# Output products of the experts in two halves, first keys by operands, three loads at other places

## What is computed

```
x = x + tanh(g_xattn) * Attn(layernorm(x), ctx, ctx)     # 16 heads of 32
    q = (query @ Wq.T) * 32**-0.5;  k = key @ Wk.T;  v = value @ Wv.T
    scores = sigmoid(q k^T);  o = scores @ v;  out = o @ Wo.T
x = x + tanh(g_ffn) * FFN(layernorm(x))
    tokens = x.reshape(8, 448, 512)                       # two batches per expert
    h = gelu(tokens @ w1[e] + b1[e])                      # 512 -> 2048
    y = h @ w2[e] + b2[e]                                 # 2048 -> 512
```

## Time and profile before

| | us |
|---|---|
| median of 3 runs | 1655.48 |
| lowest and highest | 1653.58, 1656.01 |
| the profiled execution | 1653.71 |
| its span in the profile | 1652.0 |
| PE busy | 1644.5 |
| PEld busy | 1452.0 |
| VectorE busy | 804.8 |
| ScalarE busy | 796.9 |
| POOL busy | 175.9 |

### The profile page before, as it was taken

The page is one execution under the profiler, slowest core; times in us unless marked ns, Lnnn a source line. Parts: engine busy times, 40 slices in busy tenths (PEclk is TensorE's granted clock), DMA queues, the critical chain, the costliest instruction groups (busy, mean ns, idle before and its releaser), DMA issues.

```text
span 1652.0 us, 30322 instructions
## 1 busy us (share of the span) xinstructions
PE 1644.5 (100%) x11460; PEld 1452.0 (88%) x11460; DVE 804.8 (49%) x1388; ACT 796.9 (48%) x1087; POOL 175.9 (11%) x261
## 2 busy tenths in 40 slices
PE   9999999999999999999999999999999999999999
PEld 8888888888888888888888887999999999999998
DVE  5545444443443443544443443674746565555544
ACT  6655555555555555555555556333333333333332
POOL 1212111111111111111121120000000000000000
DMA  8977687777677787786776775535344352526251
GB/s 278 265 216 217 198 222 204 195 226 206 192 220 213 194 224 204 193 237 187 210 225 186 210 227 149 203 125 180 124 168 150 131 183 98 188 93 227 94 171 48
DMA packets 195691, 309.03 MB, mean 187 GB/s; under 512 B 27088, under 2 KB 153616, under 8 KB 195568
## 3 DMA queue, kind: packets, MB, share of 16 engines
q1 hardware_dynamic: 173632, 229.43, 49.4%
q0 software_dynamic: 21936, 77.94, 13.6%
HBM read 228.44 MB, written 78.84 MB: 186 GB/s over the span
## 4 chain that ended last, share of the span: by engine, by line
PE 97%; DMA 2%; DVE 0%; SPq 0%; ACT 0%; issue 0%; POOLq 0%; DVEq 0%; ACTq 0%
PE fill_ps L686 31%; PE scores_ps L872 19%; PE fill_ps L853 14%; PE scores_ps L728 10%; PE heads_ps L745 9%; PE fill_ps L695 6%; PE heads_ps L853 5%; PE fill_ps L696 3%; DMA k_st<-k_scr 1%; DMA k_scr<-k_stage 0%; DMA probs<-WKT_in 0%; DMA part_scr<-part 0%; PE scores_ps L695 0%; SPq L404 0%; PE scores_ps L696 0%
## 5 line engine op out<-in xcount | busy, mean ns | idle before, releaser
L872 PE MATMUL scores_ps<-ctx_hl,wK 128*128 128x448 f32 x1536 | 316.6, 362 | 0.0
L872 PEld LDWEIGHTS scores_ps<-ctx_hl,wK 128*128 128x128 f32 x1536 | 288.1, 188 | 19.8
L686 PE MATMUL fill_ps<-ctx_hl,wK 128*128 128x500 f32 (+1 forms) x1560 | 287.6, 334 | 0.4 <-DVE wK L1093 0.4
L686 PE MATMUL fill_ps<-wV,ctx_hl 128*125 128x512 f32 x1152 | 280.5, 395 | 0.2 <-DVE k_stage L1201 0.2
L686 PEld LDWEIGHTS fill_ps<-ctx_hl,wK 128*128 128x128 f32 x1560 | 236.2, 189 | 31.8 <-issue 6.0
L686 PEld LDWEIGHTS fill_ps<-wV,ctx_hl 128*125 128x125 f32 x1152 | 208.9, 186 | 48.1 <-DVE k_stage L1201 0.4
L853 PE MATMUL fill_ps<-wQ,wV 128*128 128x448 f32 x1152 | 243.4, 365 | 0.0
L853 PEld LDWEIGHTS fill_ps<-wQ,wV 128*128 128x128 f32 x1152 | 216.0, 188 | 17.2 <-issue 0.4
L911 ACT ACTIVATE probs<-scores_ps 125x896 f32<-125x896 f32 x192 | 176.8, 921 | 86.7 <-PE scores_ps L728 54.4
L728 PE MATMUL scores_ps<-q_st,k_st 96*125 96x224 f32 x1536 | 200.7, 273 | 2.1 <-DMA k_st<-k_scr 2.1
L728 PEld LDWEIGHTS scores_ps<-q_st,k_st 96*125 96x125 f32 x1536 | 188.0, 188 | 16.0 <-issue 6.2
(11 more groups left out here) (120 smaller groups left out, 1706.1 us busy)
## 6 DMA issues: line engine op xcount, KB each, us to landing
k_st<-k_scr SPq DMA_DIRECT2D x576, 125.0 KB, 3.9
v_sb<-w_in SPq DMA_DIRECT2D x92, 512.0 KB, 4.6
k_scr<-k_stage POOLq DMA_DIRECT2D x62, 500.0 KB, 4.5
ctx_raw<-ctxT_in SPq DMA_DIRECT2D x48, 500.0 KB, 4.6
q_st<-q_scr SPq DMA_DIRECT2D x192, 112.0 KB, 4.0
k_scr<-k_stage POOLq DMA_DIRECT2D x68, 250.0 KB, 4.1
probs<-w_in SPq DMA_DIRECT2D x32, 512.0 KB, 3.6
q_scr<-q_stage POOLq DMA_DIRECT2D x64, 224.0 KB, 5.0
```

The lines of the kernel that those rows point to most:

```text
L686: last = pe.matmul(out_, lhsT(kt, a), rhs(kt, c), start=(kt == 0 and t == 0), stop=(kt == KT - 1 and t == 2))
L872: last = pe.matmul(y_ps[:, dt, 0:T], w2[:, slot, a, k, dt * P:(dt + 1) * P], hid_hl[:, slot, d, k, :], start=(c == 0 and k == 0 and t == 0 ...
```

## The change

Five places, none of which adds or removes arithmetic:

- `y(e, c)` becomes `y(e, c, half)`. Half 0 has the waits and output tiles 0 and 1, half 1 the tiles 2 and 3. `expert` calls half k of y(c - 1) behind tile k of chunk c.
- The first key tile (b = -1, tile 6) is computed by `first_keys`, the same 12 matmuls with the terms in the outer loop: four high by high, four high by low (context), four low (weights) by high, each term with the wait for its own operand. The waits for the low parts, which stood before the tile, are gone.
- `w_lo(2)` stands ahead of the first `leave` in VectorE's order instead of behind it.
- `load_ctx` of batch 1's first third stands at step 3 of b = -1 instead of step 1 of batch 0, and the second third takes its old place at step 1 instead of 2.
- `load_w1(0, 1)` stands at step 6 of batch 15, behind that step's gathers of keys (for step 8) and queries, instead of step 5.

```diff
@@ -88,7 +88,7 @@
 
     W_ORDER = [("K", 0), ("V", 0), ("V", 1), ("Q", 0), ("Q", 1), ("K", 1), ("O", 0), ("O", 1)]
     W_HI = {1: (3,), 2: (4,), 8: (5,), 9: (6,), 10: (7,)}
-    W_LO = {0: (2,), 4: (3,), 6: (4,), 10: (5,), 12: (6,), 13: (7,)}
+    W_LO = {-1: (2,), 4: (3,), 6: (4,), 10: (5,), 12: (6,), 13: (7,)}
     CTX_HI = {0: 1, 6: 2}
     CTX_LO = {1: 1, 7: 2}
     CTX_SPLITS = {4: 0, 5: 1, 6: 2}
@@ -430,7 +430,7 @@
                         gather_q(b + 1, 0)
                     if known(b, B - 1) and s == 0:
                         expert_start()
-                    if known(b, B - 1) and s == 5:
+                    if known(b, B - 1) and s == 6:
                         load_w1(0, 1)
                     if known(b, B - 1) and s == 9:
                         load_w1(0, 2)
@@ -438,8 +438,11 @@
                         load_w2(0, 0)
                     if s == 5 and known(b, 0):
                         load_mr(1)
-                    if attends(b) and prepares(b) and s in (1, 2, 5):
-                        load_ctx(b + 1, nh, npar, {1: 0, 2: 1, 5: 2}[s])
+                    loads = {1: 1, 5: 2} if known(b, 0) else {1: 0, 2: 1, 5: 2}
+                    if attends(b) and prepares(b) and s in loads:
+                        load_ctx(b + 1, nh, npar, loads[s])
+                    if known(b, -1) and s == 3:
+                        load_ctx(1, 0, 1, 0)
                     if s == {-1: 4, 0: 7, 1: 5}.get(b, 2) and prepares(b, 2):
                         load_xT(b + 2)
                     if known(b, 0) and s == 0:
@@ -688,6 +691,17 @@
                 return last
 
 
+            def first_keys(out_):
+                for t, (a, d, ready) in enumerate(((HI, HI, s_ctx_hi), (HI, LO, s_ctx_lo), (LO, HI, s_w_lo))):
+                    pe.wait_ge(ready, 1)
+                    if t == 0:
+                        pe.wait_ge(s_w_hi, 1)
+                    for kt in range(KT):
+                        last = pe.matmul(out_, w["K"][:, a, kt, 0:P], ctx_hl[:, 0, d, kt, :], start=(t == 0 and kt == 0),
+                                         stop=(t == 2 and kt == KT - 1))
+                return last
+
+
             def side_by_side(ps, lhsT, rhs, halves=None):
                 for kt in range(KT):
                     if halves is not None and kt % (KT // 2) == 0:
@@ -759,13 +773,13 @@
                         last = pe.transpose(ps[:, kt * LT:(kt + 1) * LT], x_rows[:, i, kt * P:(kt + 1) * P], ident[0:LT, 0:LT])
                 elif kind == "K":
                     c, mt = step_of(i) % 3, step_of(i) // 3
-                    if mt == 0:
+                    if mt == 0 and not (known(b, -1) and i == 6):
                         pe.wait_ge(s_ctx_lo, 3 * n + c + is_pair(b, i) + 1)
-                    if known(b, -1) and i == 6:
-                        pe.wait_ge(s_w_lo, 1)
                     if known(b, 0) and i == 0:
                         pe.wait_ge(s_w_lo, 6)
-                    if is_pair(b, i):
+                    if known(b, -1) and i == 6:
+                        last = first_keys(ps[:, 0:SC])
+                    elif is_pair(b, i):
                         last = three_terms(ps[:, 0:2 * SC], lambda kt, a: w["K"][:, a, kt, mt * P:(mt + 1) * P],
                                            lambda kt, a: ctx_hl[:, 0:2, a, kt, :])
                     else:
@@ -856,17 +870,18 @@
                 if half == 1 and not (known(e, 0) and (c, k) == (2, 0)):
                     last.then_inc(s_hid_full, 2 if known(e, 0) and (c, k) == (2, 1) else 1)
 
-            def y(e, c):
+            def y(e, c, half):
                 slot = c % 2
 
-                pe.wait_ge(s_ew_lo[2], C * e + c + 1)
-                pe.wait_ge(s_h_lo, C * e + c + 1)
-                if c == 0:
+                if half == 0:
+                    pe.wait_ge(s_ew_lo[2], C * e + c + 1)
+                    pe.wait_ge(s_h_lo, C * e + c + 1)
+                if half == 0 and c == 0:
 
                     at(pe, s_out, KT * e)
                     if known(e, 0):
                         pe.wait_ge(s_x1, KT * B)
-                for dt in range(KT):
+                for dt in (2 * half, 2 * half + 1):
                     for k in range(2):
                         for t, (a, d) in enumerate(TERMS):
                             last = pe.matmul(y_ps[:, dt, 0:T], w2[:, slot, a, k, dt * P:(dt + 1) * P],
@@ -879,8 +894,8 @@
                     for k in range(2):
                         if c < C and not (known(e, 0) and c < 3):
                             hidden(e, c, k)
-                    if c > 0:
-                        y(e, c - 1)
+                        if c > 0:
+                            y(e, c - 1, k)
 
             pe.wait_ge(s_ident, 2)
             turns(36)
@@ -1225,6 +1240,9 @@
                         o_lo(b - 1, 1)
                     if s == VISIT and attends(b):
                         o_lo(b, 0)
+                    if known(b, -1) and s == 0:
+                        for n in W_LO[-1]:
+                            w_lo(n)
                     for kind, i in fills_at(b, s):
                         leave(b, kind, i)
                     if known(b, -1):
```

## The result

The changed kernel took 1660.72 us (median; 1660.01 to 1661.16), the kernel before 1655.48 (1653.57 to 1656.01) in seven interleaved runs of each. The ratio is 1.0033, 95% interval 1.0023 to 1.0042: slower by 0.33%, by 5.2 us where 3.2 were forecast (1658.7). The profiled execution of the changed kernel took 1660.72 us, with a span of 1659.0; against the profiled execution of before (1653.71) that is 7.0 us. The two differences, 5.2 and 7.0, are not the same: executions of the kernel before come in two lengths, and the last experiments say why.

The account below looks back on a forecast made before the run. TensorE, with 97% of the chain of waits and no idle time in the experts, was taken as the bound. +5.8 - 0.6 - 2.1 + 0.1 = +3.2 us on the median 1655.48 gave 1658.7 us, range 1654.5 to 1661.8.

Parts of the forecast that it names:

- the halves: Output products cut in two: gaps of 0.41 at eight expert ends and 0.37 at seven starts, +5.8 us in all.
- the first keys: First key tile in order of operands: its matmuls start earlier while VectorE makes the low weights, 0.6 us gained.
- the w1 load: Last batch, load_w1(0, 1) a step later: TensorE's wait for the keys of step 8 closes, 2.1 us gained.
- T + 2.62: When the hidden split's subtraction ends, 2.62 us after T, the moment TensorE leaves a chunk's second first-layer tile.
- 0.19 of restart: After a wait, TensorE's effective start was taken to come 0.19 us after VectorE's end.
- the chain from T: From TensorE leaving a chunk's second first-layer tile: GELU, then the split's copy and subtraction, which the output product awaits; 2.61 to 2.62 us.
- gaps inside the experts: Rival: a busy queue eats the 2.0 us cover, 0.1 us in some 50 chunks; +8, 1663.5 us, chance 0.09.
- Cheaper restarts: Rival: weights load while the matmul waits, so 15 gaps cost 0.29 each; +1.7, 1657.2 us, chance 0.10.
- Late gather: Rival: last batch, step 9's keys arrive 2 us late and the gap returns there; +5.3, 1660.8 us, chance 0.09.
- The wait at 20.50: TensorE's wait for VectorE at the third value tile, claimed to move with the earlier start, keeping the 0.6 us gain.
- Context loads: Batch 1's context loads issued earlier: no gain, since ScalarE's wait at step 6 of batch 0 holds alone; bound 0.8 us.
- y(3): First expert's tightest output product, its low part ready with 0.2 us to spare: 0 to 0.2 us, counted as +0.1.

Follow-up runs that it names:

- the last experiments: Three more profiles of the unchanged kernel before, taken to see why its times spread: 1656.33, 1653.49 and 1655.84 us.
- e10_late_wait_last: Changed kernel with the output product's wait for the hidden split moved behind its wait for the output banks: 1660.96 us, ratio 1.0036 to the kernel before.
- the experiment with the shorter chain: Changed kernel, products still in halves, with the hidden split's copy and subtraction done tile by tile: 1652.34 us, ratio 0.9989 to the kernel before.
- e4_w1_only: Kernel before with load_w1(0, 1) moved from step 5 to step 6 of the last batch and nothing else: 1651.88 us, ratio 0.9981.

## Why the prediction was right, and where its terms were off

It held: the sign, the place (1660.72 in 1654.5 to 1661.8), and the mechanism with its count. The expected time was 2.0 us low, with errors of both signs: 3.0 too little for the halves and 0.6 of gain too much for the first keys on one side, 1.3 of gain too little for the w1 load on the other. Part of the nearness is luck, then. So is the class: the forecast gave slower by more than 0.2% a chance of 0.47 and no such difference 0.46, and the 0.33% measured stands clear of that edge only because the halves cost more than their sum.

- **Halves, forecast +5.8, measured +8.8** (1660.72 against 1651.92 for whole products), +8.4 in the experts of the traces. The count of 15, T + 2.62 and 0.19 of restart are as forecast where the experts are written out: 0.44 and 0.38 against 0.41 and 0.37. The step that failed is "the chain from T" being read in the first two experts alone and taken for all eight. In the loop the end costs 0.53 and the start 0.54, together 0.3 more per expert than forecast, 1.5 over five. The end's share could have been read from the trace of before, at T = 1252.31:

```profile
1252.31 9.77 PE L872 MATMUL scores_ps<-ctx_hl,wK 128*128 128x448 f32 x48
1253.93 1.09 DVE L1298 TENSOR_TENSOR ctx_hl<-q_stage,ctx_hl 128x896 fp32r<-128x896 f32 x1
```

  The subtraction ends at 1255.02, T + 2.71: VectorE's copy starts 0.11 after the end of GELU there, and 0.03 after it at the end of the first expert. The start's share, 0.24 instead of 0.11 from the signal to the product, no row of before could show; putting the late wait last took 0.1 of it away (`e10_late_wait_last`), which points to what TensorE's queue does between its two waits, without proving it. The rest, about 1 us, is pace: 0.5 in expert 7 (2.48 a tile), some 0.05 in each other one.
- **The rival "gaps inside the experts"** (0.09): none inside, as the experiment with the shorter chain and the one with halves inside alone show. **"Cheaper restarts"** (0.10): no, weight loads start with or after the wait's end. **"Late gather"** (0.09): no wait at step 9, nothing late there.
- **The w1 load, forecast -2.1**: -2.1 between the traces, -3.4 in the medians. The size of the gap was right for the execution it was read from, and 1.9 is what the median of the executions at full clock lost. What the term lacked is the fall of the clock behind the gap, some 1.6 us in nearly half of the executions; the gap itself varied from 1.56 to 2.34. The forecast had noted that the profiled execution was 1.8 us under the median, and then left that without a place. It belonged to this very gap: 1655.61 - 1653.96 = 1.65 lies between the executions with the fall and those without.
- **First keys, forecast -0.6**: nothing (1651.84 against 1651.88). "The wait at 20.50 follows a chain that starts on TensorE and moves with it" is the step that failed. It moved by 0.12. Part was gone before: the turns took until 7.84 instead of 7.50, which the kernel before hid behind VectorE's wait (over all kept traces the matmul row of the turns is 5.75 to 7.04 us long), so the values gained 0.31 and not 0.6. Then, in the trace after, ScalarE's copy of the key tile in front of it was held by the store of an earlier one:

```profile
19.51 0.37 ACT L960 CAST k_stage<-fill_ps 128x250 fp32r<-128x250 f32 x1 [1.28 <-DMA k_scr<-k_stage]
19.91 0.42 DVE L1216 TENSOR_TENSOR k_stage<-fill_ps,k_stage 128x250 fp32r<-128x250 f32 x1
```

  So the key tile waited for a free place, and a place is free when a store has landed, not when TensorE is early. That VectorE gets to the first keys some tenths later was named as the price of `w_lo(2)` and costed at nothing. No experiment had it alone, so how the rest divides between the two stays open.
- **Context loads, forecast 0**: 0 (1651.78 against 1651.88), with ScalarE's wait holding step 6 as forecast; that the keys' wait in front of it goes away wasn't forecast. **y(3)**, forecast +0.1: not separable.

On the medians the sum reads +8.8 - 3.4 = +5.4 against the +5.2 measured; the 3.4 holds for a set of runs in which most executions of before had the fall.

The faster kernel is the change without its halves: the one moved load (`e4_w1_only`, 1651.88 us, 0.19% below before), or all of the change with whole products (1651.92). If halves are wanted for another reason, the split must go by tile (1652.34).

## What to carry to other kernels

Where an engine is busy without a break, splitting a long step to interleave it with others only moves cover: compare the longest chain that hangs on the end of one piece (here T + 2.62 to 2.71) with what is left to run before its result is wanted, at the edges of a loop above all, where the interleaving partner is missing. Read that chain in each kind of code that holds it (written out and looped), and where a profiled execution lies under the median, look at the mean granted clock of the other executions before a gap is priced by its length alone.

## What the hardware showed that was not expected

- A gap of TensorE can cost more than itself. In two of four profiles of the kernel before, the granted clock went to half (0.50) for some 3 us behind a gap of 1.8 or 2.3 us and cost 1.57 us in the one worked out; in the other two a gap of 1.6 or 1.9 left it at 1.00. Of 64 executions 29 show it in their mean clock. The 15 gaps of some 0.5 in the changed kernel never did, in seven executions.
- The same 12 matmuls of a first-layer tile take 2.43 or 2.48 us, with no wait between them, and which it is is settled at a restart and stays to the next one: 0.5 us in an expert. In two kernels it alternated from expert to expert (periods of 78.36 and 78.90, of 79.57 and 80.10), and in one of them it took back more than the edit had gained.
- At an expert's end in the hardware loop the split ends 0.09 us later after T than in the written-out code (T + 2.70 against T + 2.61), because VectorE's copy starts 0.11 instead of 0.02 after GELU's end. At an expert's start in the same loop it doesn't (T + 2.63).
